# Attention on one core: one of four key chunks as fp16 halves split by GpSimd, masks made by GpSimd, VectorE's small work between masking ops

## The chip, the cores and the metric

One core of one Trainium2 chip runs the whole program. The metric is the device time of one execution in microseconds; the figure of a kernel is the median of its runs. The profile describes one further execution.

## What is computed

```python
x = x + gnn(layernorm(x), adj)          # 4096 nodes, 128 features
x = x + ffn(layernorm(x))

# gnn: two heads of 64
scores = einsum('nhd,mhd->hnm', q * SCALE, k)      # per head 4096 x 4096
scores = where(adj[None] > 0, scores, -9e15)
attn = softmax(scores, axis=-1)
sat = einsum('hnm,mhd->nhd', attn, v).reshape(N, 128)
out = leaky_relu(concat(sat[:2048] @ weightr, sat[2048:] @ weightd) + bias)

# ffn: 8 experts (128 -> 256 -> 128), gelu, the top 2 by x @ Wg + bg are added up
```

The adjacency is an int32 matrix of 4096 x 4096.

## The kernel before

Preparation: the rows are normalised, transposed, and projected to q, k (as fp16 halves: q_nat, k_half) and v (fp32, v_sb). V's eight projections (project_v) stand between those of q and k on TensorE, with a copy by ScalarE behind each.

Attention goes over 32 tiles of 128 queries. A tile has eight units, each one head h and one chunk p of 1024 keys (UNITS: units 0 and 1 are chunks 0 and 1 of head 0, 2 and 3 the same of head 1, 4 to 7 chunks 2 and 3). Every engine runs its own program, a step(i) for each tile with four rounds k of two units, and semaphores tie them. In step i

- TensorE (L945) multiplies the scores of tile i (L881: 12 fp16 matmuls for two units, two at a time on the halves of the array) into four PSUM banks, two to a unit; transposes the probabilities of tile i-1 (L896: 16 fp32 transposes of 64 x 64 blocks a unit) into banks 4 and 5, which every unit uses in turn; and multiplies them with V (attend, L912: 8 key tiles x 2 heads = 16 fp32 matmuls, which the profile counts as 32). A round is: even unit's transposes, two units' scores, odd unit's transposes, one attend.
- VectorE (L709) masks the scores and takes the row minimum in one op (mask_scores, L589), copies one half of each odd unit's transposes out of PSUM (copy_pt, L607), turns half a tile of adjacency into a mask (make_mask, L557) and does the small work behind attention for two tiles at a time (finish_tile, invert_sums, divide, leaky, residual, statistics, normalise, x2t_low, keep_logits).
- ScalarE (L443) takes the exponentials (L418) and copies the even units' transposes whole (L433) and the other half of the odd ones (L430).
- GpSimd loads the adjacency, 1024 KB to 512 KB of bf16 in a DMA (L294), takes an inverse root every second step (L329), and after the preparation splits the feed-forward weights into fp16 halves (L305, L307, L309).

A score bank is free when its unit is masked; banks 4 and 5 are free when the unit before is copied by both engines. After attention the feed-forward stage runs over eight blocks of 512 tokens; the change leaves its order alone.

## Time and profile before

| | |
|---|---|
| median of 3 runs | 851.81 us (851.72 to 851.88) |
| the profiled execution | 851.31 us |
| its span, first to last instruction | 849.5 us |
| busy: TensorE, ScalarE, VectorE, GpSimd | 96%, 80%, 75%, 23% |
| masking op L589 / half copy L607 / copy of sat_st L615 | 1219 / 688 / 289 ns mean |
| mask on VectorE L557, x64 | 759 ns mean |
| GpSimd: issue of a load L294 / inverse root L329 | 553 / 711 ns mean |
| VectorE: divide L628, L633, two of each for two tiles | 344, 347 ns mean |

Attention lasts from some 41 to 657 us, the feed-forward stage from there to the end. A busy share is a mean over the whole; what waits for what is read in a stretch.

### The profile page before, as it was taken

The numbers are of one execution on the slowest core, as the hardware profiler recorded it, in microseconds if no ns is written. First come the engines' busy times: TensorE is split into PE (matmuls) and PEld (weight loads), VectorE is DVE, ScalarE is ACT, GpSimd is POOL, SyncE is SP. The second block draws the span as 40 slices with busy tenths as digits, with TensorE's granted clock in tenths as the row PEclk, the third lists the DMA queues.
The fourth block names the chain that finished last, engine by engine and source line by source line (L and its number), as shares of the span: only waits on it lengthen the run. The fifth ranks groups of instructions, "written<-read, shape, count | busy, mean of one in ns | idle before, by whom it ended". The sixth has DMA issues, their size and how long they took to land.

```text
span 849.5 us, 31821 instructions
## 1 busy us (share of the span) xinstructions
PE 811.7 (96%) x12080; PEld 597.7 (70%) x12080; DVE 639.2 (75%) x1530; ACT 679.0 (80%) x1099; POOL 195.5 (23%) x209
## 2 busy tenths in 40 slices
PE   4969999999999999999999999999997889999997
PEld 2537777777777777777777777777776567777775
DVE  6597888888888888888888888887883465555555
ACT  4838887878788888878888888788885789999996
POOL 4180000100100010000001000000000566766774
PEclk9979999999999999999999999999999999999999
DMA  8515433443343334434333443443100000000000
GB/s 220 110 25 91 81 58 58 66 74 58 56 77 59 56 61 72 65 56 69 67 56 58 68 71 56 63 72 56 31 0 2 1 14 14 14 14 12 12 12 12
DMA packets 40900, 44.96 MB, mean 53 GB/s; under 512 B 22168, under 2 KB 32160, under 8 KB 40864
## 3 DMA queue, kind: packets, MB, share of 16 engines
q0 software_dynamic: 9216, 33.56, 24.6%
q1 hardware_dynamic: 31216, 10.71, 5.4%
q8 instruction: 24, 0.39, 0.2%
q10 hardware_dynamic: 432, 0.20, 0.1%
q14 instruction: 12, 0.10, 0.0%
HBM read 71.72 MB, written 2.10 MB: 87 GB/s over the span
## 4 chain that ended last, share of the span: by engine, by line
PE 73%; POOL 14%; issue 8%; DVE 3%; DMA 1%; ACT 0%; POOLq 0%; DVEq 0%
PE ps L912 28%; PE ps L881 19%; PE ps L896 19%; POOL prob L349 14%; PE ps L923 2%; PE ps L837 1%; PE ps L842 1%; PE ps L850 1%; DVE prob L589 1%; PE ps L931 1%; PE ps L828 1%; DMA x_sb<-in_x 1%; DVE stats L513 0%; POOLq L348 0%; ACT prob L418 0%
## 5 line engine op out<-in xcount | busy, mean ns | idle before, releaser
L589 DVE CUSTOM_DVE_ANT_0 prob<-ps,mask 128x1024 f32<-128x1024 f32 x256 | 311.8, 1219 | 90.1 <-PE ps L881 84.4
L418 ACT ACTIVATE prob<-prob,nmax 128x1024 f32<-128x1024 f32 x256 | 292.8, 1144 | 9.9 <-DVE nmax L597 9.9
L912 PE MATMUL ps<-pt,v_sb 128*64 128x128 f32 x4096 | 253.2, 277 | 0.0
L912 PEld LDWEIGHTS ps<-pt,v_sb 128*64 128x64 f32 x4096 | 222.4, 137 | 13.4 <-issue 7.5
L433 ACT ACTIVATE pt<-ps 128x1024 f32<-128x1024 f32 x128 | 131.1, 1024 | 113.0 <-PE ps L896 113.0
L896 PEld LDWEIGHTS ps<-ident,prob 64*128 64x128 f32 x4096 | 152.6, 139 | 78.5 <-issue 78.4
L881 PE MATMUL ps<-k_half,q_row 64*128 64x512 f16 x1536 | 189.7, 380 | 5.0 <-DVE low L589 5.0
L896 PE MATMUL ps<-ident,prob 64*128 64x64 f32 x4096 | 183.7, 229 | 9.4 <-issue 4.7
L349 POOL TENSOR_TENSOR prob<-prob 128x512 f16<-128x512 f32 x104 | 122.6, 1183 | 57.1 <-ACT prob L483 54.4
L294 POOL DMA_DIRECT2D mask<-in_adj x64 | 35.4, 553 | 429.2 <-DVE low L589 429.2
L791 DVE SCALAR_TENSOR_TENSOR x_sb<-ps,k_half,x_sb 128x128 f32 (+1 forms) x256 | 72.5, 344 | 78.1 <-PE ps L1029 76.8
L881 PEld LDWEIGHTS ps<-k_half,q_row 64*128 64x128 f16 x1536 | 71.5, 96 | 68.6 <-issue 9.8
L480 ACT ACTIVATE prob<-ps,b_sb 128x512 f32<-128x512 f32 x128 | 86.9, 679 | 18.3 <-PE ps L1008 16.2
L1027 PE MATMUL ps<-w_pair,prob 128*128 128x128 f16 x512 | 89.9, 220 | 6.6 <-POOL prob L349 4.7
L607 DVE COPY pt<-ps 128x512 f32<-128x512 f32 x128 | 88.0, 688 | 10.8 <-PE ps L896 9.7
L1029 PE MATMUL ps<-w_pair,prob 128*128 128x128 f16 x512 | 89.8, 220 | 0.0
L1028 PE MATMUL ps<-w_pair,prob 128*128 128x128 f16 x512 | 89.8, 220 | 0.0
L483 ACT ACTIVATE prob<-prob 128x512 f16<-128x512 f32 x128 | 80.7, 630 | 4.1
L430 ACT ACTIVATE pt<-ps 128x512 f32<-128x512 f32 x128 | 75.1, 587 | 1.8 <-PE ps L896 1.8
L1027 PEld LDWEIGHTS ps<-w_pair,prob 128*128 128x128 f16 x512 | 50.3, 98 | 14.6 <-POOL prob L349 5.4
L1028 PEld LDWEIGHTS ps<-w_pair,prob 128*128 128x128 f16 x512 | 50.4, 98 | 5.1
L1029 PEld LDWEIGHTS ps<-w_pair,prob 128*128 128x128 f16 x512 | 50.4, 98 | 0.0
(97 smaller groups left out, 670.8 us busy)
## 6 DMA issues: line engine op xcount, KB each, us to landing
mask<-in_adj POOLq DMA_DIRECT2D x64, 512.0 KB, 5.5
q_row<-q_nat SPq DMA_DIRECT2D x128, 32.0 KB, 4.7
x_sb<-in_x SPq DMA_DIRECT2D x4, 512.0 KB, 7.0
out<-x_sb SPq DMA_DIRECT2D x8, 256.0 KB, 2.3
pt<-in_L_ffn_W SPq DMA_DIRECT2D x1, 1024.0 KB, 6.5
wq_sb<-in_L_gnn_Wq ACTq DMA_DIRECT2D x1, 64.0 KB, 2.9
wk_sb<-in_L_gnn_Wk ACTq DMA_DIRECT2D x1, 64.0 KB, 4.5
wv_sb<-in_L_gnn_Wv ACTq DMA_DIRECT2D x1, 64.0 KB, 5.7
```

The source lines that it names most:

```text
L349: pool.tensor_tensor(hid_lo[:, slot, :], hid[:, slot, :], hid_hi[:, slot, :], ALU.subtract).then_inc(hid_lo_ready, 1)
L418: act.activation(prob[:, h, cols], prob[:, h, cols], ACT.Exp, bias=nmax[:, h:h + 1], scale=-1.0, accum_out=sums[:, j, h, p:p + 1]).then_in ...
L433: act.activation(pt[:, u, :, :].rearrange("p k (b q) -> p b k q", b=2), ps[:, TR0:TR0 + 2, :].rearrange("p b (k q) -> p b k q", k=KT), ACT ...
L480: act.activation(hid[:, slot, :], ps[:, (2 * e + b) % UP_BANKS, :], ACT.Gelu, bias=b1_sb[:, e, b:b + 1], scale=1.0 / W_UP).then_inc(hid_ra ...
L589: dve.tensor_tensor_reduce(out=prob[:, h, col_of(p)], in0=ps[:, 2 * (u % 2):2 * (u % 2) + 2, :].rearrange("p b c -> p (b c)"), in1=mask[:, ...
L607: dve.tensor_copy(pt[:, u, :, DH:P], ps[:, TR0 + 1, :].rearrange("p (k q) -> p k q", k=KT)).then_inc(pt_by_dve, 1)
L881: ins = pe.matmul(ps[:, 2 * (u % 2) + half, :], q_row[part, par, h, a, :], k_half[part, h, b, cols], start=first, stop=final)
L896: ins = pe.transpose(ps[:, TR0 + half, t * DH:(t + 1) * DH], prob[part, h, (p * KT + t) * P:(p * KT + t + 1) * P], ident[part, part])
L912: ins = pe.matmul(ps[dims, AV, 0:P], v_sb[:, tile, dims], pt[:, UNITS.index((h, p)), t, :], start=(tile == 0), stop=(tile == NT - 1))
L1027: pe.matmul(bank, hid_hi[:, slot, rows], w2_pair[:, 0, cols], start=(b == 0), stop=False)
L1028: pe.matmul(bank, hid_hi[:, slot, rows], w2_pair[:, 1, cols], start=False, stop=False)
L1029: ins = pe.matmul(bank, hid_lo[:, slot, rows], w2_pair[:, 0, cols], start=False, stop=(b == HB - 1))
```

## The change

- A tile's chunk 1 (units 1 and 3) is no longer multiplied in fp32. ScalarE copies it whole to pt_raw, GpSimd makes pt_hi (fp16) and pt_lo (the rest, fp16), and TensorE multiplies hi x hi, lo x hi, hi x lo: 48 fp16 matmuls. V's rows of this chunk are split once (split_values), with V scaled by 32 and the output projection by 1/32.
- The copies change parity: even units are halved between ScalarE and VectorE, odd ones are ScalarE's alone.
- Masks from tile 1 on are made by GpSimd (make_mask in its own step), between the splits and the loads.
- P times V of a tile comes one round later (AV_BLOCK 2).
- VectorE's small work moves to stand between an even and an odd masking op, spread otherwise over the two steps.
- V's projections leave the preparation for steps 0 and 1; their copies too. The weights are split by GpSimd behind step 1.

```diff
-AV_BLOCK = 1
+AV_BLOCK = 2
+SPLIT_P = 1
+SPLIT_UNITS = (1, 3)
+WHOLE = (0, 2, 4, 5, 6, 7)
...
+        pt = sb("pt", [P, len(WHOLE), KT, P], F32)
+        pt_raw = sb("pt_raw", [P, 2, KT, P], F32)
+        pt_hi = sb("pt_hi", [P, 2, KT, P], F16)
+        pt_lo = sb("pt_lo", [P, 2, KT, P], F16)
...
+            def load_adj_half(i, par, c):
+
+                if not isinstance(i, int) or i >= 2:
+                    pool.wait_ge(masked, NU * i - 12 + 4 * c)
+                cols = slice(c * HALF, (c + 1) * HALF)
+                pool.dma_start(mask[:, par, cols], adj[bass.ds(i * P, P), cols],
+                               max_dma_last_dim=8192).then_inc(adj_in[par][c], 16)
...
+            def make_mask(i, par, c):
+
+                pool.wait_ge(adj_in[par][c], 8 * i - 8 * par + 16)
+                pool.nop(nofuse=True)
+                part = mask[:, par, c * HALF:(c + 1) * HALF]
+                pool.tensor_scalar(part, part, 0.0, -BIG, ALU.is_le, ALU.mult).then_inc(mask_ready, 1)
...
+            def split_pt(j, u, early=False):
+
+                q = u // 2
+                pool.wait_ge(pt_by_act, NU * j + u + 1)
+                if not early:
+                    pool.wait_ge(av_done, NP * j + SPLIT_P - 3)
+                pool.nop(nofuse=True)
+                pool.tensor_scalar(pt_hi[:, q, :, :], pt_raw[:, q, :, :], 1.0, 0.0, ALU.mult,
+                                   ALU.add).then_inc(pt_hi_by_pool, 1)
+                pool.wait_ge(pt_hi_by_pool, 2 * j + q + 1)
+                pool.tensor_tensor(pt_lo[:, q, :, :], pt_raw[:, q, :, :], pt_hi[:, q, :, :],
+                                   ALU.subtract).then_inc(pt_by_pool, 1)
...
+            def step(i, par, prior=True, early=False, load=True, ahead=True, post=True):
+
+                if prior:
+                    split_pt(i - 1, 1, early)
+                if ahead:
+                    make_mask(i + 1, 1 - par, 0)
+                if prior:
+                    split_pt(i - 1, 3, early)
+                if load:
+                    load_adj_half(i + 2, par, 0)
+                if post and par == 0:
+                    inverse_std(i - 4)
+                if ahead:
+                    make_mask(i + 1, 1 - par, 1)
+                if load:
+                    load_adj_half(i + 2, par, 1)
...
+            step(0, 0, prior=False, post=False)
+            split_values()
+            step(1, 1, early=True, post=False)
             pool.wait_ge(w1_in, 16)
             split_weights(0, w1_raw, w1_pair)
...
+            pool.tensor_scalar(wrd[:, :, :, :], wrd[:, :, :, :], 1.0 / V_UP, 0.0, ALU.mult, ALU.add).then_inc(w_split_chain, 1)
+
+            step(2, 0, post=False)
+            step(3, 1)
+            pairs(pool, 4, NT - 2, step)
+            step(NT - 2, 0, load=False)
+            step(NT - 1, 1, load=False, ahead=False)
...
+            for j in range(V_FIRST):
+                copy_v(j)
...
+                if u % 2 == 0:
+                    act.activation(to[:, :, 0:DH], ps[:, TR0, :].rearrange("p (k q) -> p k q", k=KT),
                                    ACT.Copy).then_inc(pt_by_act, 1)
                 else:
...
+                    if post and u == 0:
+                        x2t_high(i - 5)
+                    if early and u in (1, 3, 5):
+                        copy_v(V_FIRST + u // 2)
...
+            def mask_scores(i, par, u, prior):
 
                 h, p = UNITS[u]
-                if u in (0, 4):
-                    dve.wait_ge(mask_ready, 2 * i + u // 4 + 1)
+                if u % 2 and prior:
+                    dve.wait_ge(transposed, NU * i - NU + u + 1)
+                if u in (0, 4) and isinstance(i, int) and i == 0:
+                    dve.wait_ge(mask_first, u // 4 + 1)
+                elif u in (0, 4):
+                    dve.wait_ge(mask_ready, 2 * i + u // 4 - 1)
...
                 for u in range(NU):
-                    if prior and u % 2:
+                    if finish and u == 4:
+                        finish_tile(i - 2, par)
+                    if prior and u % 2 == 0:
                         copy_pt(i - 1, u, early)
                     if now:
-                        mask_scores(i, par, u)
+                        mask_scores(i, par, u, prior)
                         if u in (5, 7):
                             row_max(i, u // 7, u)
-                    if u == 1 and finish:
-                        finish_tile(i - 2, par)
-                    if ahead and u in (3, 7):
-                        make_mask(i + 1, 1 - par, u // 4)
                     if post and par == 1:
-                        if u == 1:
+                        if u == 0 and ready:
+                            x2t_low(i - 5)
+                        if u == 2 and ready:
+                            keep_logits(i - 5)
+                        if u == 4:
                             invert_sums(i - 3)
-                        if u == 3:
+                        if u == 6:
                             divide(i - 3)
-                        if u == 5:
-                            leaky(i - 3)
-                        if u == 7:
-                            residual(i - 3)
                     if post and par == 0:
-                        if u == 1:
+                        if u == 0:
+                            leaky(i - 4)
+                        if u == 2:
+                            residual(i - 4)
                             statistics(i - 4)
-                        if u == 3:
+                        if u == 6:
                             normalise(i - 4)
-                        if u == 5:
-                            x2t_low(i - 4)
-                        if u == 7:
-                            keep_logits(i - 4)
+                    if last and u == 2:
+                        rank_gates(0, 0, RANKED_EARLY)
...
+                if p == SPLIT_P:
+                    pe.wait_ge(pt_by_pool, 2 * j + 2)
+                else:
+                    pe.wait_ge(pt_by_act, NU * j + ready)
...
+                    if p == SPLIT_P:
+                        for values, probs in ((0, pt_hi), (0, pt_lo), (1, pt_hi)):
+                            for h in range(HEADS):
+                                dims = slice(h * DH, (h + 1) * DH)
+                                ins = pe.matmul(ps[dims, AV, 0:P], v_pair[:, values, t, dims], probs[:, h, t, :],
+                                                start=False, stop=False)
...
+                    if not prior:
+                        project_v(k)
+                    if not prior and k == 3:
+                        project_v(k + 1)
                     if prior:
                         transposes(i - 1, 2 * k + 1, early)
-                    if post and par == 1 and k == 1:
+                    if early and k < NC - V_FIRST:
+                        project_v(V_FIRST + k)
+                    if post and par == 1 and k == 2:
                         out_project(i - 3)
-                    if post and par == 0 and k == 2:
-                        x2_transpose(i - 4)
-                    if post and par == 0 and k == 3:
-                        logits(i - 4)
                     if k >= AV_BLOCK and prior:
                         attend(i - 1, k - AV_BLOCK, early)
                     elif k < AV_BLOCK and drain:
                         attend(i - 2, k + NP - AV_BLOCK)
+                    if post and par == 0 and k == 3:
+                        x2_transpose(i - 4)
+                    if post and par == 1 and k == 0 and ready:
+                        logits(i - 5)
...
-            for p in range(NP - AV_BLOCK, NP):
-                attend(NT - 1, p)
+            attend(NT - 1, NP - 2)
+            logits(NT - 2 * PAIR)
+            attend(NT - 1, NP - 1)
```

VectorE, second round of an even step: from the masking op to the next one. Before (what follows the masking op of unit 1, with the small work behind the odd unit):

```order
L589 ISA prob,low<-ps,mask 128x1024
L589 ISA low 128x1
L612 ISA
L615 COPY sat_st<-ps 128x128
L652 ISA
L652 BN_STATS stats<-x_sb 128x6
L652 ISA
L652 BN_STATS stats<-x_sb 128x6
L654 REGISTER_ALU
L657 BN_AGGR mv<-stats 128x2 x2
L659 REGISTER_ALU
L660 TENSOR_SCALAR ve<-mv 128x2
```

After (from unit 2's masking op; L663 is masking, L718 the residual add, L724 to L732 the statistics):

```order
L663 ISA prob,low<-ps,mask 128x1024
L663 ISA low 128x1
L718 ISA
L718 TENSOR_TENSOR x_sb<-x_sb,o_act 128x256
L572 REGISTER_ALU
L724 BN_STATS stats<-x_sb 128x6
L724 ISA
L724 BN_STATS stats<-x_sb 128x6
L726 REGISTER_ALU
L729 BN_AGGR mv<-stats 128x2 x2
L731 REGISTER_ALU
L732 TENSOR_SCALAR ve<-mv 128x2
```

The residual and the statistics now stand between units 2 and 3; the adjacency masks are gone from this engine.

GpSimd, the loop over pairs of steps, its even step. Before, from the inverse root on:

```order
L329 TENSOR_TENSOR rstd<-ve,expo 128x2
L292 ISA
L294 ISA
L294 DMA mask<-in_adj 128x2048
L292 REGISTER_ALU
L294 ISA
L294 DMA mask<-in_adj 128x2048
```

After (L333 and L336 are the two halves of the split, L316 the mask, L308 the load):

```order
L333 TENSOR_SCALAR pt_hi<-pt_raw 128x1024
L335 ISA
L336 TENSOR_TENSOR pt_lo<-pt_raw,pt_hi 128x1024
L313 ISA
L316 TENSOR_SCALAR mask<-mask 128x2048
L329 REGISTER_ALU
L333 TENSOR_SCALAR pt_hi<-pt_raw 128x1024
L335 REGISTER_ALU
L336 TENSOR_TENSOR pt_lo<-pt_raw,pt_hi 128x1024
L306 ISA
L308 ISA
L308 DMA mask<-in_adj 128x2048
```

A mask stands between the splits of unit 1 and unit 3, and each load behind a split or a mask.

GpSimd around the end of the weight split. Before, its last rows and the first loads behind it:

```order
L309 TENSOR_TENSOR w_pair<-pt,w_pair 128x2048
L305 TENSOR_SCALAR wg_sb<-wg_sb 128x8
L307 TENSOR_SCALAR wg_pair<-wg_sb 128x8
L309 TENSOR_TENSOR wg_pair<-wg_sb,wg_pair 128x8
L305 TENSOR_SCALAR b_sb<-b_sb 8x128
L307 TENSOR_SCALAR b_pair<-b_sb 8x128
L309 TENSOR_TENSOR b_pair<-b_sb,b_pair 8x128
L324 TENSOR_SCALAR ident<-ident 128x128
L294 DMA mask<-in_adj 128x2048 x8
```

After, the same rows and what follows, which is GpSimd's part of step 2:

```order
L351 TENSOR_TENSOR w_pair<-x2t_lo,w_pair 128x2048
L347 TENSOR_SCALAR wg_sb<-wg_sb 128x8
L349 TENSOR_SCALAR wg_pair<-wg_sb 128x8
L351 TENSOR_TENSOR wg_pair<-wg_sb,wg_pair 128x8
L347 TENSOR_SCALAR b_sb<-b_sb 8x128
L349 TENSOR_SCALAR b_pair<-b_sb 8x128
L351 TENSOR_TENSOR b_pair<-b_sb,b_pair 8x128
L393 TENSOR_SCALAR ident<-ident 128x128
L394 TENSOR_SCALAR wrd<-wrd 128x512
L333 TENSOR_SCALAR pt_hi<-pt_raw 128x1024
L336 TENSOR_TENSOR pt_lo<-pt_raw,pt_hi 128x1024
```

The splits and masks of step 2 are queued behind the weights, which themselves stand behind step 1's loads.

## Rows read from the trace of the kernel before

**Rows 1.** Busy time by stretch: window, length, busy by engine with counts, granted clock, DMA

```profile
27.37:33.77 6.40, 6.40 (x38) 3.78 (x37) 4.19 (x11) 5.84 (x13) 0.00 (x0) 1.00 1.03 203
100.00:200.00 100.00, 100.00 (x1673) 75.61 (x1674) 84.58 (x182) 80.89 (x132) 8.20 (x14) 1.00 0.40 66
640.00:650.00 10.00, 7.42 (x113) 6.60 (x115) 2.90 (x10) 6.72 (x12) 0.69 (x1) 0.83 0.01 2
```

**Rows 2.** Chain in order of time, attention loop: start, us, what

```profile
304.02 0.59 PE ps L896 x16
304.61 1.90 PE ps L912 x32
306.51 0.65 PE ps L896 x16
307.16 1.29 PE ps L881 x12
...
314.00 0.03 PE ps L941
```

**Rows 3.** Timeline, ScalarE, attention loop: start, us, instruction, shapes, count

```profile
303.69 1.14 ACT L418 ACTIVATE prob<-prob,nmax 128x1024 f32<-128x1024 f32 x1
...
304.83 0.59 ACT L430 ACTIVATE pt<-ps 128x512 f32<-128x512 f32 x1
...
307.27 1.02 ACT L433 ACTIVATE pt<-ps 128x1024 f32<-128x1024 f32 x1 [0.73 <-PE ps L896]
```

**Rows 4.** Timeline, VectorE, attention loop

```profile
302.57 0.48 DVE L652 BATCH_NORM_STATS2 stats<-x_sb 128x6 f32 x2
...
303.71 1.23 DVE L589 CUSTOM_DVE_ANT_0 prob<-ps,mask 128x1024 f32<-128x1024 f32 x1
...
304.87 0.69 DVE L607 COPY pt<-ps 128x512 f32<-128x512 f32 x1
305.47 1.21 DVE L589 CUSTOM_DVE_ANT_0 prob<-ps,mask 128x1024 f32<-128x1024 f32 x1
...
307.95 1.22 DVE L589 CUSTOM_DVE_ANT_0 prob<-ps,mask 128x1024 f32<-128x1024 f32 x1
```

**Rows 5.** Groups by line and form: busy us, mean ns (the residual add)

```profile
L646 DVE TENSOR_TENSOR x_sb<-x_sb,o_act 128x256 f32 x13 | 5.4, 418 | 0.0
```

**Rows 6.** Timeline, GpSimd, weight split

```profile
40.77 1.90 POOL L305 TENSOR_SCALAR pt<-pt 128x2048 f32<-128x2048 f32 x1 [18.31 <-DVE k_half L550]
...
44.74 4.07 POOL L309 TENSOR_TENSOR w_pair<-pt,w_pair 128x2048 f16<-128x2048 f32 x1
...
59.55 0.29 POOL L324 TENSOR_SCALAR ident<-ident 128x128 f16<-128x128 f32 x1
```

**Rows 7.** Timeline, VectorE, during the weight split

```profile
46.85 2.50 DVE L557 TENSOR_SCALAR mask<-mask 128x2048 bf16<-128x2048 bf16 x1
...
51.79 1.23 DVE L589 CUSTOM_DVE_ANT_0 prob<-ps,mask 128x1024 f32<-128x1024 f32 x1
...
54.28 3.53 DVE L557 TENSOR_SCALAR mask<-mask 128x2048 bf16<-128x2048 bf16 x1
```

**Rows 8.** Timeline, VectorE, both inputs in SBUF: end of attention, feed-forward stage

```profile
637.59 1.69 DVE L699 TENSOR_TENSOR k_half<-k_half 128x28 f32<-128x28 f32 x7
...
686.97 4.87 DVE L699 TENSOR_TENSOR k_half<-k_half 128x4 f32<-128x4 f32 x7
```

**Rows 9.** Timeline, GpSimd, feed-forward stage, same time

```profile
686.77 2.40 POOL L349 TENSOR_TENSOR prob<-prob 128x512 f16<-128x512 f32 x2 [0.24 <-ACT prob L483]
```

**Rows 10.** Timeline, TensorE: preparation, end of attention, feed-forward stage

```profile
33.77 1.95 PE L850 MATMUL ps<-wv_sb,prob 128*128 128x128 f32 x16
...
642.78 3.53 PE L912 MATMUL ps<-pt,v_sb 128*64 128x128 f32 x32
...
666.51 0.22 PE L1028 MATMUL ps<-w_pair,prob 128*128 128x128 f16 x1
666.56 0.22 PE L1029 MATMUL ps<-w_pair,prob 128*128 128x128 f16 x1
```

More of the change, by code:

```diff
@@ L229, in build @@
         N_QKV_W, N_W = 3, 8
-        W_SPLITS = 13
+        W_SPLITS = 14
         @block.sync
@@ L324, in _ @@
             pool.tensor_scalar(ident16[:, :], ident[:, :], 1.0, 0.0, ALU.mult, ALU.add).then_inc(w_split_chain, 1)
-            def inverse_std(t0):
-                pool.wait_ge(ve2_ready, t0 + PAIR)
-                pool.tensor_tensor(rstd2[:, :], ve2[:, :], expo[:, 0:PAIR], ALU.pow).then_inc(rstd2_ready, PAIR)
-            def load_behind_post(i, par):
-                if par == 0:
-                    inverse_std(i - 6)
-                load_adj(i, par)
-            for i in range(2, 6):
-                load_adj(i, i % 2)
-            pairs(pool, 6, NT, load_behind_post)
-            for t0 in range(NT - 6, NT, PAIR):
-                inverse_std(t0)
+            pool.tensor_scalar(wrd[:, :, :, :], wrd[:, :, :, :], 1.0 / V_UP, 0.0, ALU.mult, ALU.add).then_inc(w_split_chain, 1)
[4 more added lines that the diff above has]
+            step(NT - 1, 1, load=False, ahead=False)
+            step(NT, 0, load=False, ahead=False)
+            inverse_std(NT - PAIR)
             def ffn(j, par):
@@ L460, in _ @@
             step(3)
-            pairs(act, 4, NT, lambda i, par: step(i, post=par == 0))
-            step(NT, now=False, post=True, last=True)
+            step(4)
+            step(5, post=True)
+            pairs(act, 6, NT, lambda i, par: step(i, post=par == 1))
+            step(NT, now=False, last=True)
+            x2t_high(NT - 2 * PAIR)
             act.wait_ge(b1_in, 16)
@@ L744, in _ @@
             step(2, 0, post=False)
-            step(3, 1)
-            pairs(dve, 4, NT - 2, step)
+            step(3, 1, ready=False)
+            step(4, 0)
+            step(5, 1)
+            pairs(dve, 6, NT - 2, step)
             step(NT - 2, 0)
             step(NT - 1, 1, ahead=False)
-            rank_gates(0, 0, RANKED_EARLY)
-            step(NT, 0, now=False, ahead=False)
+            step(NT, 0, now=False, ahead=False, last=True)
             choose_gates(0, 0, RANKED_EARLY)
+            x2t_low(NT - 2 * PAIR)
+            keep_logits(NT - 2 * PAIR)
             finish_tile(NT - 1, 1)
@@ L836, in project_qk @@
                         pe.wait_ge(q_lo_ready, j - 1)
-                    pe.matmul(ps[:, j % 2, :], wq_sb[:, :], xn_t[:, j % 4, :], start=True, stop=True).then_inc(q_psum, 1)
+                    pe.matmul(ps[:, j % 2, :], wq_sb[:, :], xn_t[:, j, :], start=True, stop=True).then_inc(q_psum, 1)
                 for h in range(HEADS):
@@ L943, in logits, with step @@
                 ins.then_inc(logit_psum, PAIR)
-            def step(i, par, prior=True, now=True, drain=True, post=True, early=False):
+            def step(i, par, prior=True, now=True, drain=True, post=True, ready=True, early=False):
                 for k in range(NU // 2):
@@ L971, in _ @@
             pe.wait_ge(w_split_chain, W_SPLITS)
-            step(3, 1)
-            pairs(pe, 4, NT, step)
+            step(3, 1, ready=False)
+            step(4, 0)
+            step(5, 1)
+            pairs(pe, 6, NT, step)
             step(NT, 0, now=False)
-            for p in range(NP - AV_BLOCK, NP):
-                attend(NT - 1, p)
+            attend(NT - 1, NP - 2)
+            logits(NT - 2 * PAIR)
+            attend(NT - 1, NP - 1)
             def gate_transpose(j):
```

112 lines of the change are left out of this document (61 added, 51 removed).

## The prediction, made before the change was timed

> **What bounds the kernel now.** I read the busy table of a stretch in the middle of attention first: TensorE is busy for 100 of 100 us, VectorE for 85, ScalarE for 81, GpSimd for 8 [rows 1]. So between about 63 and 634 us TensorE never waits, and only what shortens its own work, or starts to make it wait, moves the end. The chain in order of time gives one round of the attention loop [rows 2]: a block of P times V 1.90 us, an even unit's transposes 0.65, two units' scores 1.29, an odd unit's transposes 0.59: 4.43 us, four rounds a step, and the small projections beside them.
>
> The other engines follow this beat. ScalarE, in a round, has two exponentials (1.14 each), a half copy (0.59) and a whole copy (1.02), 3.9 of 4.43 [rows 3]. VectorE's masking op starts 0.79 us after an even unit's transposes end (307.16 [rows 2], 307.95 [rows 4]) and takes 1.16 to the next start, its half copy 0.60 (303.71, 304.87, 305.47 [rows 4]). GpSimd is nearly idle here.
>
> **The fp16 chunk.** One of four blocks of P times V per step goes from 16 fp32 matmuls (32 records, 1.90 us, 59 ns each) to 48 fp16 ones. Scores, which run in pairs on the two halves of the array, take 12 in 1.29 us, 108 ns each for 512 columns; a quarter of that for 128 columns is 27 ns, and 48 make 1.29 us. A block of many short matmuls hardly keeps to that scale, so I add a tenth: 1.42. The loads of the 8-column matmuls lie 0.03 us apart (the piece at 314.00 [rows 2]), 48 x 0.03 = 1.44, so loads don't forbid it. I take 1.45, a gain of 0.45 us a step (bounds 0.3 and 0.6); over 31 steps in which TensorE sets the beat **-14 us** (-9 to -19). The worst end is a pair that doesn't overlap: in the feed-forward stage one 128-column fp16 matmul follows the other by 0.05 to 0.06 us (666.51, 666.56 [rows 10]), 48 of them at 0.055 are 2.66 us, +0.76 a step. That is a rival below.
>
> **GpSimd's new load.** Per step two high halves, two low halves, two masks, two DMA issues. Its one-input op over 2048 elements takes 1.90 us and over 128 elements 0.29, so 1024 take 1.04; the subtraction over 2048 takes 4.07, so 1024 take about 2.1 [rows 6]. No row shows a mask made on GpSimd: the bounds are 1.9 (the one-input op of as many elements) and 4.07 (the two-input one), and I take 1.9, since it has one input. Sum: 2 x (1.04 + 2.1) + 2 x 1.9 + 1.1 + 0.7 in every second step = some 11.5 us of 17.9: it keeps up in the mean. The split of unit 3 is ready about 12 us after the step's first transposes, the fp16 block wants it at 3 x 4.43 + 1.88 = 15.2. So in the steady state this wait is covered by about 3 us.
>
> **VectorE.** It loses two masks a step (0.69 us each) and keeps four half copies. Its small work now stands between the even and the odd masking op. The new wait of the odd masking op on its unit's transposes is met at 1.88 us and costs nothing, since VectorE gets there at 1.95. From an even unit's transposes: masking ends at 0.79 + 1.16 = 1.95, small work w, the odd masking op 1.16, then the next half copy. That copy must start by 4.43 + 0.6, or TensorE waits at the odd transposes (they come 1.29 after the even ones, the copy takes 0.6, a semaphore 0.1). In the even step's second round w is largest: residual 0.42 [rows 5] and statistics from 302.57 to 303.71, 1.14 [rows 4]. That ends at 4.7, with the 0.2 of the saturated tile's copy 4.9: just in time. The divide of the odd step, about 1.3, stands before a round shortened to 4.0 and costs 0 to 0.1. Taken alone: **0** (0 to 3 us over all).
>
> **The clash.** What the rows show is that VectorE and GpSimd stop each other for some ops. Making half a mask (0.69 us alone, 0.76 in the mean of all 64) took 2.50 and 3.53 us while GpSimd split weights, and ended as GpSimd's op did (the subtraction from 44.74 [rows 6] ends at 48.8); a masking op beside them took its usual 1.23 [rows 7]. Masking reads one tensor in PSUM and one in SBUF. And seven tiny tensor_tensor ops, both inputs in SBUF, took 4.87 us together while GpSimd subtracted, against 1.69 for seven larger ones with GpSimd idle [rows 8, 9]. The residual add, x_sb plus o_act, is of that kind. The Trainium skill says so of both ("SBUF — State Buffer", Who interferes with whom): a VectorE instruction with two SBUF inputs and a GpSimd instruction that reads SBUF lock each other out for the whole instruction. The trace agrees; if the rule didn't hold here, the sum would be without the term that follows.
>
> Where do they meet? Count from the end of unit 1's transposes. ScalarE copies the whole unit (0.05 + 1.02 + 0.08), GpSimd splits (1.04 + 0.08 + 2.1) and begins the first mask half at 4.4. VectorE: attend 1.90 and unit 2's transposes 0.65, then 0.79 + 1.16: the residual comes at 4.5. It is 0.1 us late for an op of 1.9, so it waits 1.8. Then the odd masking op ends at 9.05 and the half copy starts at 9.3 after the small copy; latest without a loss was 2.55 + 4.43 + 0.6 = 7.58. TensorE stands for 1.7 us. Even steps 4 to 30 do this, 14 of them: **+24 us** (bounds: 0 where VectorE comes first; 14 x 3.9 = 55 where the mask takes 4.07). The leaky op also has two SBUF inputs, but runs at 2.0 to 2.4 us of the step, before GpSimd starts at 3.0.
>
> **The start.** V's eight projections leave the preparation, where they were on TensorE's way. A pair takes 1.95 us on TensorE (33.77 [rows 10]), in rounds of 6.40 in which TensorE never idles and ScalarE is busy for 5.84 [rows 1]. Without the pair TensorE would need 4.5, ScalarE (without two V copies of about 0.55) 4.75, and with its waits about 5: 1.4 saved in each of two rounds, 1.4 in what lies before and after them together. I take -4.2 to the first score matmul. The two stretched masks go from VectorE: -1.8 in step 0 (2.50 less 0.69), -2.8 in step 1. The first exponential, however, waits on ScalarE behind five V copies, and three projections (0.95 each) fall into step 1: +2.8. Sum **-6** (-3 to -8).
>
> **The weight split.** Before, GpSimd splits the weights from 40.77 to 59.84, 19.1 us [rows 6], in which nobody needs it but for the masks above. Now it does that after the last load of step 1, which waits for all of that step's masking, so from 0.2 us before step 2's count begins to 19.0; then split 3.2, mask 1.9, split 3.2 ready at 27.3. Step 2's fp16 block is due at 15.2. Queued behind this wait on TensorE are all later scores and transposes, so nothing covers it: **+12 us** (+8 to +14), and after such a pause TensorE works more slowly for a while: over 640 to 650, with pauses, the granted clock was 0.83 in the mean against 1.00 [rows 1], and the block at 642.78 took 3.53 us [rows 10] where the chain has 1.90: **+2** (0 to 3).
>
> **The end.** One more block (AV_BLOCK 2) stands behind the last transposes, and the logits of tiles 28 and 29: **+1.5** (0 to 3). The feed-forward stage keeps its order: 0.
>
> **The sum.** 849.5 (span of the profiled execution) - 14 + 0 + 24 - 6 + 12 + 2 + 1.5 = 869; that execution took 851.31 with 1.8 outside the span, so 870.8; the median of the runs is 0.5 above it: **871 us**.
>
> **Rivals.**
> - *VectorE comes first, or the two don't stop each other.* The margin of 0.1 us is smaller than what I can read off. The residual then runs at once, GpSimd's mask waits 0.4, which it can afford: no term of 24, 847 us, faster than before. For it: both ends of the race hang on the same transposes, so it falls the same way in all 14 steps. Against: every op ahead of the mask on GpSimd has a row. Chance 0.23 (842 to 852).
> - *The residual is free, but a later op of the chain is stopped.* VectorE's tiny variance op (128 x 2) comes about 0.9 us before the mask ends; the fast mask op of [rows 7] shows that one-input ops can be stopped too. It loses 0.8 in each of 14 steps: 847 + 11 = 858. By the Trainium skill ("VectorE: DVE Perf Modes", What auto-detection actually checks) an op with one source in SBUF and an even outermost dimension takes the mode that uses both ports; no row here shows it for this op beside a busy GpSimd. Chance 0.15 (852 to 863).
> - *The mask is dear on GpSimd*, 3.5 to 4 us: the residual waits 2.2 longer, 871 + 30 = 901; at 3 us 885. Chance 0.10.
> - *The fp16 pairs don't overlap*: 1.2 us a step worse than reckoned, 871 + 37 = 908. Chance 0.04; the fp32 pairs on the same halves do overlap.
>
> **How the numbers follow.** The forecast has 0.45 (863 to 879), 0.03 is left for what I don't see. From 845 to 885 lie all of the forecast, all of the second rival and most of the first, some 0.8. The measurement tells 0.2% from no change, so faster is below 850.1 and slower above 853.5. Faster: most of the first rival, 0.20. Same: 0.04. Slower: 0.76.
>
> **What would show it.** In the changed profile: an fp16 block of 1.45 us in the chain (gain), a gap of about 12 us on TensorE near 85 us whose releaser is GpSimd's pt_lo, and in even steps the residual add with about 2.2 us instead of 0.42, beginning just after a mask on GpSimd, with TensorE idle 1.7 us before the next odd unit. If that add keeps 0.42 the first rival holds; if the variance op is long, the second; if the mask's mean is over 3 us, the third. I am wrong altogether if TensorE also waits elsewhere in each step, say for GpSimd's split or a mask that comes late.

## The result, and the profile after

| | before | after |
|---|---|---|
| median | 851.85 us (851.72 to 851.89, 4 runs) | **1066.03 us** (1065.53 to 1066.08, 4 runs) |
| span of the profiled execution | 849.5 us | 1063.8 us |
| ratio | | 1.2508 [1.2489, 1.2527] |

The change costs 214 us, where 19 were forecast; 1066 lies far outside the range of 845 to 885. The page of the kernel after (busy table, GpSimd's and TensorE's clock rows in 40 slices; then two groups: line, engine, what it writes and reads, count, busy us, mean ns, idle before):

```profile
PE 845.3 (79%) x12592; PEld 628.3 (59%) x12592; DVE 729.9 (69%) x1468; ACT 691.9 (65%) x1099; POOL 841.8 (79%) x403
...
POOL 3499997979798887979797979797978316666775
PEclk9997798989889897979898979789997988999999
...
L316 POOL TENSOR_SCALAR mask<-mask 128x2048 bf16<-128x2048 bf16 x62 | 440.0, 7097 | 9.3 <-DMA mask<-in_adj 8.7
...
L336 POOL TENSOR_TENSOR pt_lo<-pt_raw,pt_hi 128x1024 f16<-128x1024 f32 x64 | 137.5, 2148 | 5.3
...
L333 POOL TENSOR_SCALAR pt_hi<-pt_raw 128x1024 f16<-128x1024 f32 x64 | 66.7, 1042 | 73.5 <-ACT pt_raw L496 72.9
```

The first thing to see is the mask: **7.10 us for half a tile on GpSimd**, 62 times, where the forecast took 1.9 and VectorE needed 0.76. The two splits cost what [rows 6] said, 1.04 and 2.15. The same stretch of attention, before (in [rows 1] a part of it) and after (window, length, busy us with counts of TensorE, its weight loads, VectorE, ScalarE, GpSimd, granted clock, DMA):

```profile
150.00:600.00 450.00, 450.00 (x7478) 338.55 (x7478) 378.12 (x808) 366.69 (x592) 34.87 (x60) 1.00 0.39 63
```

```profile
150.00:600.00 450.00, 354.41 (x5837) 269.77 (x5835) 336.07 (x561) 278.62 (x437) 392.67 (x153) 0.88 0.29 47
```

GpSimd goes from 35 to 393 us of 450, TensorE from 450 to 354, and its granted clock from 1.00 (2.4 GHz) to a mean of 0.88, which means pieces at the lower level. A pair of steps (start of one inverse root on GpSimd to the next; after, ten intervals from 159.26 to 663.04) takes 50.4 us after and 37.35 before: 13 us in each of about 15 pairs are 196 of the 214. TensorE's part of a pair: it idles 10.7 us (95.6 x 50.4 / 450) and is busy for 39.7 instead of 37.35, although the fp16 blocks are shorter than the fp32 ones: the rest is the lower clock.

The pairs are of two kinds. In 150 to 600 two of nine look like this one, VectorE (start, us, instruction):

```profile
297.78 2.37 DVE L718 TENSOR_TENSOR x_sb<-x_sb,o_act 128x256 f32 x1
...
301.19 5.93 DVE L732 TENSOR_SCALAR ve<-mv 128x2 f32<-128x2 f32 x1
...
315.28 3.57 DVE L738 TENSOR_SCALAR x<-x_sb,mv,rstd 128x128 f32 x2
```

and GpSimd beside it:

```profile
297.72 2.15 POOL L336 TENSOR_TENSOR pt_lo<-pt_raw,pt_hi 128x1024 f16<-128x1024 f32 x1
299.84 7.25 POOL L316 TENSOR_SCALAR mask<-mask 128x2048 bf16<-128x2048 bf16 x1
307.07 1.03 POOL L333 TENSOR_SCALAR pt_hi<-pt_raw 128x1024 f16<-128x1024 f32 x1
...
311.60 7.10 POOL L316 TENSOR_SCALAR mask<-mask 128x2048 bf16<-128x2048 bf16 x1
```

Read the ends. The residual add (0.42 in [rows 5]) begins with GpSimd's subtraction and ends at 300.15, just after it. The variance op, 128 x 2, begins at 301.19 and ends at 307.12, as the mask from 299.84 does (307.09). The two normalisations end at 318.85, the mask from 311.60 at 318.70. So in this kind of pair three small VectorE ops wait for GpSimd, and the long masks make two of these waits long. TensorE pays with it:

```profile
307.30 1.47 PE L955 MATMUL ps<-k_half,q_row 64*128 64x512 f16 x6 [6.49 <-DVE low L663]
...
309.54 3.15 PE L1000 MATMUL ps<-pt,v_sb 128*64 128x128 f32 x32
...
318.91 0.69 PE L1020 MATMUL ps<-ident,x 128*128 128x128 f32 x2 [2.32 <-DVE x L738]
```

The scores after the pause run at 1.47 for six (12 in 1.46 otherwise), the block of P times V takes 3.15 instead of 1.97.

The other seven pairs go another way (VectorE, GpSimd, TensorE):

```profile
348.86 0.98 DVE L732 TENSOR_SCALAR ve<-mv 128x2 f32<-128x2 f32 x1
361.42 7.20 DVE L738 TENSOR_SCALAR x<-x_sb,mv,rstd 128x128 f32 x2 [4.21 <-POOL rstd L356]
```

```profile
360.66 0.73 POOL L356 TENSOR_TENSOR rstd<-ve,expo 128x2 f32<-128x2 f32 x1
361.37 7.10 POOL L316 TENSOR_SCALAR mask<-mask 128x2048 bf16<-128x2048 bf16 x1
```

```profile
368.68 0.69 PE L1020 MATMUL ps<-ident,x 128*128 128x128 f32 x2 [5.68 <-DVE x L738]
```

Here the variance op meets only the end of a subtraction and takes 0.98. VectorE then stands 4.21 us for the inverse root, which GpSimd reaches late, behind the first mask and the split of unit 3. GpSimd's second mask stands right behind the root, so the two normalisations, which need the root, meet that mask from its start and take 7.20 instead of 0.60.

The three largest waits of TensorE in 150 to 600 (total, times, longest) add up to 95.0 of its 95.6 us of idle time:

```profile
PE ps L1020 <- DVE x L738: 46.8, 9, 6.6
...
PE ps L995 <- POOL pt_lo L336: 28.5, 16, 3.3
...
PE ps L955 <- DVE low L663: 19.7, 9, 6.5
```

So both things stand in the profile: VectorE ops stopped by GpSimd (66.5 us, with the late inverse root in seven of the nine pairs as a part of it), and GpSimd itself late with the splits (28.5). What a pair of steps would cost if only one of them were there is not to be read from it; the experiments are for that.

### The profile page after: what moved, and what is told of

Its sections match the earlier page's. It is cut to its first block, busy times and chain, and to the rows that moved or that the text cites. A ratio compares the mean times of both kernels' runs of the same rounds, so it can differ in the third digit from the quotient of the medians.

```text
span 1063.8 us, 33247 instructions
## 1 busy us (share of the span) xinstructions
PE 845.3 (79%) x12592; PEld 628.3 (59%) x12592; DVE 729.9 (69%) x1468; ACT 691.9 (65%) x1099; POOL 841.8 (79%) x403
## 4 chain that ended last, share of the span: by engine, by line
POOL 30%; PE 28%; issue 25%; DVE 10%; ACT 2%; POOLq 1%; DVEq 0%; ACTq 0%
POOL prob L410 11%; POOL mask L316 10%; PE ps L955 9%; PE ps L1000 8%; PE ps L970 7%; DVE x L738 4%; POOL pt_hi L333 3%; DVE prob L663 2%; POOL pt_lo L336 2%; ACT pt_raw L496 2%; PE ps L995 1%; PE ps L1020 1%; POOL mask L308 1%; DVE x_sb L718 1%; PE ps L1012 1%
## 5 line engine op out<-in xcount | busy, mean ns | idle before, releaser
L316 POOL TENSOR_SCALAR mask<-mask 128x2048 bf16<-128x2048 bf16 x62 | 440.0, 7097 | 9.3 <-DMA mask<-in_adj 8.7
L663 DVE CUSTOM_DVE_ANT_0 prob<-ps,mask 128x1024 f32<-128x1024 f32 x256 | 313.7, 1238 | 42.9 <-PE ps L970 14.3
L1000 PE MATMUL ps<-pt,v_sb 128*64 128x128 f32 x3072 | 196.1, 282 | 0.0
L1000 PEld LDWEIGHTS ps<-pt,v_sb 128*64 128x64 f32 x3072 | 172.9, 141 | 11.1 <-issue 5.1
L336 POOL TENSOR_TENSOR pt_lo<-pt_raw,pt_hi 128x1024 f16<-128x1024 f32 x64 | 137.5, 2148 | 5.3
L333 POOL TENSOR_SCALAR pt_hi<-pt_raw 128x1024 f16<-128x1024 f32 x64 | 66.7, 1042 | 73.5 <-ACT pt_raw L496 72.9
L738 DVE TENSOR_SCALAR x<-x_sb,mv,rstd 128x128 f32 (+1 forms) x32 | 91.1, 4017 | 45.6 <-POOL rstd L356 45.6
L995 PE MATMUL ps<-pt_hi,v_pair 128*64 128x128 f16 x1024 | 60.2, 246 | 70.2 <-POOL pt_lo L336 70.2
L995 PEld LDWEIGHTS ps<-pt_hi,v_pair 128*64 128x64 f16 x1024 | 54.6, 127 | 73.5 <-issue 73.2
L1123 PE MATMUL ps<-w_pair,prob 128*128 128x128 f16 x512 | 90.3, 221 | 6.6 <-POOL prob L410 4.7
L496 ACT ACTIVATE pt<-ps 128x1024 f32<-128x1024 f32 x64 | 65.5, 1023 | 45.0 <-PE ps L970 42.8
L1125 PE MATMUL ps<-w_pair,prob 128*128 128x128 f16 x512 | 90.1, 221 | 0.0
```

Source lines behind the costliest of these rows:

```text
L316: pool.tensor_scalar(part, part, 0.0, -BIG, ALU.is_le, ALU.mult).then_inc(mask_ready, 1)
L333: pool.tensor_scalar(pt_hi[:, q, :, :], pt_raw[:, q, :, :], 1.0, 0.0, ALU.mult, ALU.add).then_inc(pt_hi_by_pool, 1)
L336: pool.tensor_tensor(pt_lo[:, q, :, :], pt_raw[:, q, :, :], pt_hi[:, q, :, :], ALU.subtract).then_inc(pt_by_pool, 1)
L663: dve.tensor_tensor_reduce(out=prob[:, h, col_of(p)], in0=ps[:, 2 * (u % 2):2 * (u % 2) + 2, :].rearrange("p b c -> p (b c)"), in1=mask[:, ...
L738: ins = dve.tensor_scalar(x2[:, t, :], x_sb[:, bass.ds(t0 + t, 1), :].rearrange("p t d -> p (t d)"), mv2[:, t, 0:1], rstd2[:, t:t + 1], AL ...
L995: ins = pe.matmul(ps[dims, AV, 0:P], v_pair[:, values, t, dims], probs[:, h, t, :], start=False, stop=False)
```

## The experiments

### What an op costs on GpSimd

The kernel before, with ten one-input ops over 128 x 2048 ahead of its GpSimd program, on scratch buffers; nothing is left out.

```diff
+ for o, i_, s1, s2, p1, p2 in ((h_in, h_in, 0.0, -BIG, le, mu), (h_out, h_in, 0.0, -BIG, le, mu),
+                               (h_out, h_in, BIG, -BIG, mu, ad), (h_out, h_in, 1.0, BIG, ALU.subtract, mu),
+                               (f_out, f_in, 0.0, -BIG, le, mu), (f_out, f_in, BIG, -BIG, mu, ad),
...
+     pool.tensor_scalar(o, i_, s1, s2, p1, p2).then_inc(forms, 1)
```

> The kernel before with ten one-input GpSimd ops over 128 x 2048 elements put ahead of everything, on scratch, each waiting for the one in front: what the mask costs by itself. The forms are bf16 or fp32 in and out, with the compare (is_le, mult) of the mask or with plain arithmetic (mult, add). If the compare makes the mask dear, the compare forms take 7.1 us in every type and the arithmetic ones 1.9; if bf16 does, all forms that touch bf16 take 7.1 and the fp32 compare 1.9; if neither alone, the mask takes 1.9 here and its 7.1 in the changed kernel is contention with VectorE. The output is the reference's; the time says nothing but that some 40 us stand in front.

GpSimd's busy time in windows that hold one op each, in the order of the code (columns: window, length, GpSimd busy with count, clock, DMA):

```profile
5.70:12.85 7.15, 7.12 (x1) 1.00 1.17 304
12.90:20.00 7.10, 7.08 (x1) 1.00 0.90 208
20.00:22.00 2.00, 1.90 (x1) 1.00 0.19 1
22.00:29.20 7.20, 7.09 (x1) 1.00 0.00 0
29.20:36.35 7.15, 7.09 (x1) 1.00 0.00 0
36.35:38.35 2.00, 1.90 (x1) 1.00 0.00 0
```

Compare then multiply 7.1 us, subtract then multiply 7.1, multiply then add **1.90**, in bf16 as in fp32, in place or not; the four ops with mixed types, left out here, read 1.90, 7.08, 1.90, 7.08. So not the type, and not VectorE beside it (from 22 us on it does nothing in these windows, and the times are the same), but the **pair of operations** sets the time. A second ladder of the same make asks which pairs are quick: (multiply, multiply), (add, multiply), (add, add), (multiply, subtract), (max, min), then single compare, multiply, add, subtract.

> The kernel before with nine more one-input GpSimd ops over 128 x 2048 bf16 elements on scratch ahead of everything. The first ladder had 1.9 us for (mult, add) and 7.1 for (is_le, mult) and (subtract, mult), in every type. Here, in this order: (mult, mult), (add, mult), (add, add), (mult, subtract), (max, min), then single ops is_le, mult, add, subtract. If only the one pair (mult, add) is fast, all the others take 7.1 or some value of their own; if it is compares and a leading subtract that are slow, the arithmetic pairs take 1.9. The output is the reference's; the time says nothing.

```profile
5.70:7.70 2.00, 1.90 (x1) 1.00 1.20 290
7.70:9.65 1.95, 1.90 (x1) 1.00 1.20 290
9.65:16.85 7.20, 7.10 (x1) 1.00 1.10 314
16.85:24.05 7.20, 7.11 (x1) 1.00 0.35 37
24.05:31.20 7.15, 7.09 (x1) 1.00 0.00 0
31.20:36.70 5.50, 5.38 (x1) 1.00 0.00 0
36.70:42.10 5.40, 5.37 (x1) 1.00 0.00 0
```

Of the pairs tried only multiply-add, add-multiply and multiply-multiply take 1.90; the rest take 7.1, and every single operation 5.37 (the last two, left out, too): a multiply with nothing behind it is dearer than a multiply by 1 and an add of 0. The split's high half is written as (multiply, add), which is why it, and the row of [rows 6] that I priced the mask by, were cheap. Neither of the two outcomes named for this ladder came: not only one pair is quick, and not all arithmetic pairs are. Why these three are quick, no run here shows.

### The mask in the quick form

The mask is 0 where the adjacency is 1 and -BIG where it is 0, so for the inputs here x BIG - BIG gives the same.

```diff
-                pool.tensor_scalar(part, part, 0.0, -BIG, ALU.is_le, ALU.mult)
+                pool.tensor_scalar(part, part, BIG, -BIG, ALU.mult, ALU.add)
```

> The changed kernel, its mask on GpSimd made by mult and add (adjacency x BIG - BIG, the same values for 0 and 1) in place of compare and mult. If the compare is what is dear, a mask takes 1.9 us, and this is the kernel that was forecast: 871 us (845 to 885), with the residual add blocked behind the first mask in even steps. If bf16 is what is dear, masks stay at 7.1 us and the time at 1066.

**869.21 us** (866.55 to 870.65), ratio 1.0187 [1.0166, 1.0208]: 197 of the 214 us are gone with one line. A pair takes 37.52 us, the mask 1938 ns:

```profile
L316 POOL TENSOR_SCALAR mask<-mask 128x2048 bf16<-128x2048 bf16 x49 | 95.0, 1938 | 0.4
```

That is 2 us beside my 871, but not by my sum. VectorE and GpSimd where they meet:

```profile
318.60 0.47 DVE L718 TENSOR_TENSOR x_sb<-x_sb,o_act 128x256 f32 x1
...
320.12 0.73 DVE L732 TENSOR_SCALAR ve<-mv 128x2 f32<-128x2 f32 x1
```

```profile
318.75 2.08 POOL L316 TENSOR_SCALAR mask<-mask 128x2048 bf16<-128x2048 bf16 x1
```

The residual add is 0.15 us ahead of the mask, not 0.1 behind, and keeps its time. The mask then runs at once, and the variance op stops until its end: the second rival. It costs TensorE 0.50 us before the next scores (TensorE waits for VectorE's low in 20 places, 7.2 us in 150 to 600, this one among them). And the pause that was forecast is there, followed by a block at the lower clock (the fp16 block lasts from 101.43 to 104.14, 2.7 us, at a granted clock of 0.50, which is 1.2 GHz):

```profile
101.43 0.32 PE L995 MATMUL ps<-pt_hi,v_pair 128*64 128x128 f16 x2 [12.96 <-POOL pt_lo L336]
...
104.14 1.11 PE L970 MATMUL ps<-ident,prob 64*128 64x64 f32 x16
```

### Is it the place of the mask?

The kernel after, with both splits ahead of both masks on GpSimd.

```diff
-                if ahead:
-                    make_mask(i + 1, 1 - par, 0)
                 if prior:
                     split_pt(i - 1, 3, early)
+                if ahead:
+                    make_mask(i + 1, 1 - par, 0)
```

> The changed kernel with both splits of a GpSimd step ahead of both masks, same work. Before the change a pair of steps takes 37.3 us, in the changed kernel 50.4, of which GpSimd is busy for 44.5. If it is the place of the first mask between the splits that delays the fp16 block, the pair falls to about GpSimd's own 44.5, the time to 975 us (960 to 1000). If VectorE's stopped ops (residual, variance, normalise) set the beat, it stays within 2% of 1066, for they meet a mask wherever it stands.

**1077.56 us** (1076.66 to 1079.0), ratio 1.2642 [1.2621, 1.2663], a pair 51.2 us. Serving the splits first doesn't help: TensorE's wait for pt_lo is gone from 150 to 600, but in all nine pairs VectorE now stands some 4.2 us for the inverse root behind the first mask, and the normalisation then meets the second:

```profile
315.93 7.19 DVE L738 TENSOR_SCALAR x<-x_sb,mv,rstd 128x128 f32 x2 [4.23 <-POOL rstd L356]
```

```profile
315.87 7.11 POOL L316 TENSOR_SCALAR mask<-mask 128x2048 bf16<-128x2048 bf16 x1
```

In this kernel the wait of TensorE's transposes L1020 for it is 92.4 us in 150 to 600 (9 times, up to 10.3), against 46.8 in the kernel after. The work was moved in GpSimd's queue and the loss moved with it; other orders were not tried.

### Masks back on VectorE

```diff
-                if ahead:
-                    make_mask(i + 1, 1 - par, 0)
...
+                    if ahead and u in (3, 7):
+                        make_mask(i + 1, 1 - par, u // 4)
```

(out of GpSimd's step, into VectorE's.)

> The changed kernel with the masks made by VectorE again, behind units 3 and 7 as in the kernel before; GpSimd only splits and loads. If the masks on GpSimd are the whole of the loss, what is left is the fp16 chunk's gain (0.5 us a step, 14 us to 17), the weight split's pause (+12), the start (-4) and what VectorE loses to its new order and to the splits: 850 to 870 us. If GpSimd's splits are themselves too late or stop VectorE as much, it stays above 890.

**902.58 us** (901.23 to 907.71), ratio 1.0608 [1.0572, 1.0644]. GpSimd is busy for only 181 of 450 us, and yet this is 33 us slower than the quick mask on GpSimd, and slower than I expected. The mask on VectorE meets the splits (VectorE, then GpSimd, then TensorE):

```profile
335.12 1.69 DVE L623 TENSOR_SCALAR mask<-mask 128x2048 bf16<-128x2048 bf16 x1
336.73 0.28 DVE L683 COPY sat_st<-ps 128x128 f32<-128x128 f32 x1
336.93 0.68 DVE L675 COPY pt<-ps 128x512 f32<-128x512 f32 x1
```

```profile
334.13 2.13 POOL L336 TENSOR_TENSOR pt_lo<-pt_raw,pt_hi 128x1024 f16<-128x1024 f32 x1
```

```profile
337.75 0.71 PE L968 MATMUL ps<-ident,prob 64*128 64x64 f32 x16 [1.59 <-DVE pt L675]
338.40 3.43 PE L998 MATMUL ps<-pt,v_sb 128*64 128x128 f32 x32
```

One of the two masks of a step is stopped like this (1.46 or 1.69), the other keeps its 0.68. 0.68 becomes 1.69 (the subtraction ends at 336.26, and the mask with its own work soon after), the half copy behind it is late, TensorE waits 1.59, and the next block runs for 3.43 us instead of 1.97. TensorE waits 23.7 us for that copy in 150 to 600; the rest is the lower clock behind the waits (mean 0.98). How much each of the two adds to the 33 us I did not separate.

### The weights first, and the variance op away

Three kernels from the one with the quick mask. The first splits the feed-forward weights before GpSimd's step 1, after tile 1's masks:

```diff
-            step(0, 0, prior=False, post=False)
-            split_values()
-            step(1, 1, early=True, post=False)
+            for c in range(2):
+                make_mask(1, 1, c)
             pool.wait_ge(w1_in, 16)
...
+            for c in range(2):
+                load_adj_half(2, 0, c)
+            split_values()
+            step(1, 1, early=True, post=False)
```

> The kernel with the mult and add mask (869.2 us), the weight split moved ahead of GpSimd's part of step 1 (both masks of tile 1 before it). In that kernel TensorE stood for 12.96 us in step 2, waiting for the first split behind the weights. If that pause is the whole price of the place, it goes, with the slower clock behind it: 854 to 857 us. If GpSimd's first splits or tile 2's masks now come late instead, part of it comes back in steps 1 and 2: above 860.

**854.71 us** (853.99 to 857.66), ratio 1.0035 [1.0022, 1.0047]. The pause is gone; the pair stays at 37.52. So the pause with the slow clock behind it costs 14.5 us (forecast 12 + 2). The runs of the quick mask spread over 4 us, so this difference and the next hold to about 2.

The second gives the variance op to GpSimd, ahead of the inverse root, where it takes 0.18 us:

```diff
+                pool.tensor_scalar(ve2[:, :], mv2[:, :, 1], 1.0, EPS, ALU.mult, ALU.add).then_inc(ve2_ready, PAIR)
...
-                dve.tensor_scalar(ve2[:, :], mv2[:, :, 1], EPS, None, ALU.add).then_inc(ve2_ready, PAIR)
```

> The kernel with the mult and add mask (869.2 us), VectorE's variance op left to GpSimd (mult 1, add eps, on 128 x 2, just ahead of the inverse root). That op takes 0.73 us on VectorE there instead of 0.17, stopped by GpSimd, and stands ahead of a masking op. A pair of steps takes 37.5 us; TensorE's own work would be 36.3. If the stopped op is the term, 0.6 to 0.8 us a pair go: 858 to 861 us. If the odd step's divide or the residual add holds TensorE, it is 866 to 869.

**860.53 us** (858.0 to 861.39), ratio 1.0093 [1.0075, 1.0111]; pair 36.86 instead of 37.52, 0.66 in each of some 14, which is 9 us, against 8.7 between the medians.

> Both edits together. If the pause and the late half copies are independent, the gains add: 844 to 848 us, faster than the kernel before (0.991 to 0.996). If one only uncovers the other, 853 or more.

Both edits: **847.07 us** (846.62 to 847.32), ratio 0.993 [0.9913, 0.9948], pair 36.86. The two gains add up (14.5 + 8.7 = 23.2 against 22.1), and the changed design is now 0.7% faster than the kernel before, little, but clear of the noise.

### The same stop with the dear mask

The variance op moved as above, but in the kernel after, with its 7.1 us masks.

> The changed kernel with its 7.1 us masks, and only the variance op left to GpSimd. There that op takes 5.93 us in an even step and TensorE waits 6.5 us behind it. If VectorE's stopped ops set the beat, up to 5.5 us a pair go: 985 to 1000 us. If GpSimd's own queue does (the fp16 block waits for a split behind a mask), most of it comes back as a wait for the split: 1030 to 1060.

**1074.82 us** (1073.06 to 1075.54), ratio 1.2595 [1.2573, 1.2618]: slower than the kernel after, and a miss of my expectation. That was read off the one pair shown first, with 5.93 us for the variance op; such a stop comes in two of nine pairs only. Now all nine are of the other kind, VectorE first 5.5 us idle for the inverse root and then in the normalisation, which meets the next mask from its start:

```profile
315.52 7.19 DVE L738 TENSOR_SCALAR x<-x_sb,mv,rstd 128x128 f32 x2 [5.50 <-POOL rstd L358]
```

```profile
315.47 7.08 POOL L316 TENSOR_SCALAR mask<-mask 128x2048 bf16<-128x2048 bf16 x1
```

TensorE's wait for pt_lo also grows, from 28.5 to 42.8 us in 150 to 600. So both ops go: the normalisation also leaves VectorE (ScalarE does it as an activation with a scale and a shift that GpSimd prepares).

```diff
+                pool.tensor_scalar(neg2[:, :], mv2[:, :, 0], -1.0, 0.0, ALU.mult, ALU.add).then_inc(neg2_ready, PAIR)
...
+                pool.tensor_tensor(shift2[:, :], neg2[:, :], rstd2[:, :], ALU.mult).then_inc(shift2_ready, PAIR)
...
+                    ins = act.activation(x2[:, t, :], x_sb[:, bass.ds(t0 + t, 1), :].rearrange("p t d -> p (t d)"),
+                                         ACT.Identity, bias=shift2[:, t:t + 1], scale=rstd2[:, t:t + 1])
...
-                        if u == 6:
-                            normalise(i - 4)
```

> The changed kernel with its 7.1 us masks on GpSimd, but VectorE free of the two ops that were seen stopped longest: the variance op goes to GpSimd and the normalise to ScalarE (two activations behind unit 7 of an even step, with a shift that GpSimd computes). The residual add stays. If VectorE being stopped set the beat, a pair of steps falls from 50.4 us to GpSimd's own 45 to 47, the time to 985 to 1015 us. If GpSimd's queue alone sets it (masks ahead of the splits, and the load that waits for all of a step's masking), the pair stays at 49 to 51 and the time at 1045 to 1070.

**996.06 us** (994.54 to 998.67), ratio 1.1692 [1.1661, 1.1723], pair 45.4 us. Now GpSimd hardly rests (442 of 450 us):

```profile
150.00:600.00 450.00, 378.10 (x6444) 291.17 (x6444) 295.24 (x590) 316.10 (x503) 441.68 (x199) 0.94 0.32 52
```

```profile
PE ps L1011 <- POOL pt_lo L340: 57.4, 20, 4.2
```

(the second view is that of the waits, TensorE's largest in that stretch.) This parts the 13 us of a pair: with both ops off VectorE (the residual add stays), GpSimd's own work (4 masks at 7.1, 4 splits at 3.2, the issues and the inverse root: 44.5 us) still holds the pair at 45.4. **Some 8 us are GpSimd as the bound, some 5 are VectorE held up by it**, stopped in an op or idle for the inverse root; no run parts these two. Both the 8 and the 5 hang on the 7.1. ScalarE's normalisation isn't free either: TensorE waits 9.9 us in the 450 for it.

### The best version

Both edits and the quick mask, with the residual add one round earlier, behind the leaky op, so that it can't meet GpSimd's first mask:

```diff
                             leaky(i - 4)
-                        if u == 2:
                             residual(i - 4)
+                        if u == 2:
                             statistics(i - 4)
```

> The kernel with both edits (847.07 us), the residual add moved one round earlier, behind the leaky op. In that kernel a pair of steps takes 36.86 us where TensorE's own work is some 36.3; the second round of an even step is the one whose half copy is just in time. If that is the rest of the loss, 0.2 to 0.5 us a pair go: 840 to 845 us. If it is the odd step's divide, the time stays within 1 us.

**843.97 us** (842.26 to 845.29), ratio 0.9892 [0.9864, 0.9919], pair 36.65. The time is as expected, the cause isn't shown: TensorE idles as long as with both edits alone (8.4 and 8.5 us in 150 to 600), so the 0.2 us a pair are not the wait that I meant to take away. In its chain the fp16 block stands as forecast (start, us, what):

```profile
303.29 1.90 PE ps L1003 x32
...
307.62 1.46 PE ps L998 x48
```

## Why the prediction was wrong, point by point

**The step that failed** is the price in "GpSimd's new load": "No row shows a mask made on GpSimd: the bounds are 1.9 (the one-input op of as many elements) and 4.07 (the two-input one), and I take 1.9, since it has one input." It measured 7.10, outside both bounds. The number of inputs was the wrong thing to be near to: all one-input rows of the kernel before on GpSimd are (multiply, add), and the mask is (compare, multiply). The Trainium skill ("GPSIMD Engine Reference", Engine selection) puts an op with one input at roughly line rate there; the rows at 7.1 us for 2048 elements a partition speak against it as a rule for every operation. The bounds came from two rows of the same kind of arithmetic, and nothing in the trace bounded another kind; that should have widened the third rival, which named the very mechanism and stopped at 4 us.

**What followed from it.** "It keeps up in the mean", with 11.5 us of 17.9: measured 22 of 25 (and 17.9 was itself low: a step takes 18.7 before and 18.3 in the best version). The cover of 3 us over the split wait in the steady state was gone, and TensorE waits for pt_lo in 16 places, about as many as there are steps (28.5 us in 450). The third rival's sum (901) let only the residual wait longer; it left out that GpSimd becomes the bound, some 8 us a pair, and that GpSimd's late inverse root would hold up VectorE.

| term | forecast | measured | from |
|---|---|---|---|
| fp16 block | 1.45 us | 1.46 us | chain of the best version |
| fp16 pairs don't overlap (rival) | 0.04 | no | the same |
| mask on GpSimd | 1.9 | 7.10; 1.94 in the quick form | kernel after; quick mask |
| clash with the residual add | 1.7 us a pair | 0: VectorE first by 0.15 us | quick mask |
| variance op stopped (rival 2) | 0.8 a pair | 0.66 a pair | variance op moved |
| VectorE's own order | 0 (0 to 3 over all) | 0.5 a pair, some 7 over all | best version |
| pause for the weight split, with its clock | 12 + 2 | 14.5 | weights first |
| the start | -6 | about 0 | below |
| VectorE held up beside dear masks | not foreseen beyond the residual add | 5 us a pair | kernel without the stops |

**The clash.** The mechanism, VectorE ops with both inputs in SBUF stop and are stopped by GpSimd, is seen (0.42 becomes 2.37 beside the subtraction in the kernel after). I had the add 0.1 us behind the mask, it is 0.15 ahead, so the race for which the sum had 24 us fell the other way, as the first rival said; then the second rival came true, 0.73 us for the variance op. That the forecast of 871 stands 2 us from the kernel with the quick mask is chance: 24 too much for the clash is made up by 9 for the variance op, 6 for a start that brought nothing, and some 7 for half copies that come late. The second rival had the right mechanism for this kernel, and its 858 missed by 11 us.

**The start.** In the kernel with the quick mask the first score matmul comes 3.1 us earlier (38.09 for 41.22), not 4.2. In the kernel after it doesn't (41.26): VectorE's own mask for tile 0, 0.69 us alone, is stopped by GpSimd's first mask, takes 6.15, and the k halves behind it are late. With the quick mask the span is 19.3 above the one of before; the pause takes 14.5 of it (15.9 by the spans of the two profiled executions) and the steady pairs 2.6 (15 x 0.17), so 1 to 2 are left for start and end together, where -6 and +1.5 were forecast. What eats the 3.1 before step 2 was not tried.

**The steady gain.** The block alone gives 0.44 x 2 = 0.88 a pair; the best version's pair is 0.70 shorter. What still waits in it is TensorE for VectorE's half copy (5.9 us in 150 to 600, 0.5 a pair), namely the one behind the odd step's divide (0.53 in the pair at 330.56). The prediction gave that divide "0 to 0.1" and "VectorE taken alone: 0 (0 to 3 us over all)"; it is some 7 over 15 pairs, so this term was too small.

**The weight split** was right in place, size and cause. In the kernel after the pause is 23.8 us, since 7.1 us masks lie behind the split as well.

## What to carry to other kernels

Before work moves to GpSimd, time that very operation there, with the operations of its two stages and not only its shape and number of inputs: a factor of 3.7 lay between two ways to write one mask. Then list VectorE's ops that share time with it: residual adds, one-number ops and normalisations are stopped for as long as GpSimd's instruction lasts, so each such instruction should be short, and moving one op out of its way can put the next one in. Look at several turns of a loop before you take one for typical: the stop of 5.93 us in the pair read first comes in two of nine. And one-off work on a queue belongs ahead of the loop's first request, not behind.

## What the hardware showed beyond this

- GpSimd over 128 x 2048: 1.90 us for (multiply, add), (add, multiply), (multiply, multiply); 7.1 for (compare, multiply), (subtract, multiply), (add, add), (multiply, subtract), (max, min); 5.37 for a single compare, multiply, add or subtract. For (compare, multiply) and (multiply, add) bf16 or fp32 makes no difference; the others were run in bf16 only.
- An op of 128 x 2 on VectorE was stopped for 5.8 us, and two normalisations of 128 x 128, which read one tensor and two per-partition numbers from SBUF, for 6.6 (7.19 against 0.60). The Trainium skill ("SBUF — State Buffer", Who interferes with whom) lets copies, casts and tensor-scalar ops in the modes with two ports take part in the lock beside ops with two SBUF inputs; both rows agree with it, and the prediction had priced that only as a rival.
- The masking op, one input in PSUM, kept its 1.20 to 1.23 us beside GpSimd in all kernels; only where it stands behind the stopped variance op does its record read 2.68, in three places of the kernel after, and there both records end together.
- Waits cost more than themselves: after 6.49 us of idling, six score matmuls took 1.47 us at a granted clock of 0.50 (1.2 GHz, 307.30 to 308.53), where twelve take 1.46 otherwise; over 150 to 600 the granted clock was 0.88 in the mean.
